# The masked key copies of a 16-wide self attention moved ahead of the query and product copies on ScalarE

## The reference

```python
q = (x @ w_q + b_q).reshape(B, Lq, 16, 16)          # x normalised; Lq = 256, B = 16
k = (context @ w_k + b_k).reshape(B, -1, 16, 16)    # 120 keys of context
v = (context @ w_v + b_v).reshape(B, -1, 16, 16)
scores = einsum('bqhd,bkhd->bhqk', q, k) / 4
weights = softmax(scores, axis=-1)
out = einsum('bhqk,bkhd->bqhd', weights, v).reshape(B, Lq, D)
x = x + out @ w_o + b_o
```

## Time and profile before

| what | us |
|---|---|
| median of three runs | 5142.15 (5141.17 to 5146.36) |
| the profiled execution's own time | 5143.89 |
| its span in the trace | 5142.0 |
| PE busy over the span | 4271.9 (83%) |
| DVE busy | 3517.8 (68%) |
| ACT busy | 2240.1 (44%) |
| POOL busy | 492.5 (10%) |
| the stage's first and last instruction in the trace | about 562 to 907 |

### The profile page before, as it was taken

How to read it: one execution, slowest core, us unless ns; L and a number is a source line. 1 busy time by engine, 2 the same in 40 slices (tenths; PEclk the granted TensorE clock), 3 DMA queues, 4 the chain that set the end, 5 groups by cost and what they waited for, 6 DMA issues and landing times. The chain is left out here.

```text
span 5142.0 us, 72988 instructions
## 1 busy us (share of the span) xinstructions
PE 4271.9 (83%) x23248; PEld 3274.5 (64%) x23248; DVE 3517.8 (68%) x8249; ACT 2240.1 (44%) x5337; POOL 492.5 (10%) x921
## 2 busy tenths in 40 slices
PE   6993588799879999999999999999514787787786
PEld 5771477577647777777777777778302555555554
DVE  4656666666667777777777777777754777777445
ACT  2331366455436555555555555655240222222322
POOL 0002100101130000000000000000301121121300
PEclk9995799899979999999999999999655888888689
DMA  2000000000000000000000000000002000000101
GB/s 59 0 0 22 33 0 0 1 0 0 12 6 1 4 1 4 3 2 4 2 4 2 4 2 4 2 2 1 3 11 59 0 0 0 0 0 0 36 0 33
DMA packets 33742, 41.23 MB, mean 8 GB/s; under 512 B 5116, under 2 KB 29954, under 8 KB 33414
## 3 DMA queue, kind: packets, MB, share of 16 engines
q1 hardware_dynamic: 33480, 38.08, 2.5%
HBM read 33.61 MB, written 4.19 MB: 7 GB/s over the span
## 5 line engine op out<-in xcount | busy, mean ns | idle before, releaser
L1563 DVE TENSOR_TENSOR global_prob_t_low<-psum,global_prob_t_high 128x512 fp32r<-128x512 f32 x960 | 657.1, 690 | 252.2 <-ACT global_prob_t_high L1655 238.0
L1655 ACT ACTIVATE global_prob_t_high<-psum 128x512 fp32r<-128x512 f32 x960 | 569.9, 601 | 586.9 <-PE psum L1769 586.9
L1569 DVE TENSOR_REDUCE global_top<-psum 128x1 f32<-128x480 f32 x1024 | 666.1, 657 | 109.2 <-PE psum L1729 104.2
L1676 ACT ACTIVATE global_prob<-psum,global_bias 128x480 f32<-128x480 f32 x1024 | 674.2, 662 | 17.9 <-DVE global_bias L1572 15.1
L1769 PE MATMUL psum<-ident,global_prob 128*128 128x128 f32 x3840 | 568.3, 273 | 37.1 <-DVE global_prob_t_low L1563 36.1
L1769 PEld LDWEIGHTS psum<-ident,global_prob 128*128 128x128 f32 x3840 | 467.4, 141 | 196.1 <-DVE global_prob_t_low L1563 68.7
L1727 PE MATMUL psum<-global_prob_t_high,global_v_low 128*128 128x512 f32 x960 | 455.7, 475 | 0.9
L1727 PE MATMUL psum<-global_k_high,global_q_low 128*128 128x480 f32 x1024 | 390.2, 381 | 15.6 <-ACT global_prob L1676 13.1
L1729 PE MATMUL psum<-global_k_high,global_q_high 128*128 128x480 f32 x1024 | 391.3, 382 | 0.0
L1728 PE MATMUL psum<-global_k_low,global_q_high 128*128 128x480 f32 x1024 | 388.3, 379 | 0.0
L1728 PE MATMUL psum<-global_prob_t_low,global_v_high 128*128 128x512 f32 x960 | 379.4, 395 | 0.0
(11 more groups left out here) (439 smaller groups left out, 8147.2 us busy)
## 6 DMA issues: line engine op xcount, KB each, us to landing
x_res<-in_x SPq DMA_DIRECT2D x4, 1024.0 KB, 9.6
moe_we<-in_expert_t SPq DMA_DIRECT2D x8, 512.0 KB, 7.6
out<-x_res SPq DMA_DIRECT2D x4, 1024.0 KB, 8.7
cho_wqkv<-in_L_ffn_Wqkv SPq DMA_DIRECT2D x2, 1536.0 KB
self_ctx_t<-in_ctx_t SPq DMA_DIRECT2D x2, 1440.0 KB
sel_w<-in_L_xattn_W SPq DMA_DIRECT2D x2, 1024.0 KB, 11.9
global_ctx_t<-in_ctx_t SPq DMA_DIRECT2D x1, 1440.0 KB
sel_ctx_t<-in_ctx_t SPq DMA_DIRECT2D x1, 1440.0 KB
```

Of the source, the lines that this page charges most:

```text
L1563: dve.tensor_tensor(dst, psum, high.bitcast(F32), ALU.subtract).then_inc(ready.sem, 1)
L1569: ins = dve.tensor_reduce(top[:, c:c + 1], w.psum[:, c, 0:chunk], AX.X, ALU.max)
L1655: act.activation(dst, psum, ACT.Copy).then_inc(ready.sem, 1)
L1676: act.activation(prob[:, par, j, c * chunk:(c + 1) * chunk], w.psum[:, c, 0:chunk], ACT.Exp, bias=bias[:, j % 2:j % 2 + 1], scale=scale, a ...
```

## The change

On ScalarE, in odd turns, the wait for `k_psum` and the four key copies (L437) with their signal `k_ready` move from behind the copy of the product (L431) to directly behind the exponential (L420), ahead of the wait for `q_psum` and the two query copies (L426) and ahead of the wait for `share_psum` and L431. No instruction is added, removed or given another shape, and no other engine's program changes.

```diff
                         act.activation(prob[:, s, :, :, :, :].rearrange("p m r a j -> p r m (a j)"),
                                        w.psum[:, 0:groups, 0:cols * NCTX].rearrange("p r (m c) -> p r m c", m=parts),
                                        ACT.Exp, scale=scale).then_inc(exped.sem, 1)
+                    if s == 1 and exists(3):
+                        act.wait_ge(k_psum.sem, k_psum.count(batch + 2))
+                        for m in range(parts):
+                            for a in range(pair):
+                                last = act.activation(k_t[:, m, a, :], kv_cols[:, m * NCTX:(m + 1) * NCTX],
+                                                      ACT.Identity, bias=bk_masked[:, m, a:a + 1],
+                                                      scale=mask[:, a:a + 1])
+                        last.then_inc(k_ready.sem, 1)
                     if exists(3):
                         act.wait_ge(q_psum.sem, q_psum.count(t + 3))
...
                         act.wait_ge(share_psum.sem, share_psum.count(t + 1))
                         act.activation(attn_raw[:, :, :], attn_cols.rearrange("p (k t) -> p k t", t=P),
                                        ACT.Copy).then_inc(attn_kept.sem, 1)
-                    if s == 1 and exists(3):
-                        act.wait_ge(k_psum.sem, k_psum.count(batch + 2))
-                        for m in range(parts):
-                            for a in range(pair):
-                                last = act.activation(k_t[:, m, a, :], kv_cols[:, m * NCTX:(m + 1) * NCTX],
-                                                      ACT.Identity, bias=bk_masked[:, m, a:a + 1],
-                                                      scale=mask[:, a:a + 1])
-                        last.then_inc(k_ready.sem, 1)
```

## The result

| | before | changed |
|---|---|---|
| median, us | 5142.11 (5141.17 to 5146.36, 5 runs) | 5121.01 (5118.20 to 5122.57, 5 runs) |
| profiled execution's span, us | 5142.0 | 5119.4 |
| PE busy over the span, us | 4271.9 | 4265.7 |

The ratio is 0.9957 (95% interval 0.9942 to 0.9971): 21 us faster by the medians, 22.6 us by the two spans. The forecast was 5118.2 us with a range of 5112 to 5126.

What follows compares the result with a forecast made beforehand. PE was taken to bound the stage, waiting 2.02 us a pass for key copies. Savings of 20.4 + 1.53 + 0.58 + 1.37 = 23.9 us took the median from 5142.15 to 5118.2 us, range 5112 to 5126.

Steps and rivals of the forecast that it cites:

- The wait and its size: PE's scores L467 wait for key copies L437 once each loop pass, 2.02 us each, 28.3 us in 14 waits.
- How long the blocks last: ScalarE's key copies start 0.337 us apart, so first key copy to first query copy takes 1.35 us.
- A pass: In a loop pass PE's scores start 1.57 us sooner (bounds 1.53 and 1.71), leaving some 0.45 us wait for queries.
- The ends of the stage: Turns outside the thirteen regular ones: turn 27 saves 1.53 us, turn -1 0.58 us, turn -3 1.37 us.
- Turn -3: Stage's start, no exponential: key copies fit before the queries, which wait for L534 as before; saves 1.37 us.
- turn -1: Near the stage's start, where the queries had waited for nothing: scores start at 594.63 against 595.21, saving 0.58 us.
- What is later than before: Queries come 0.97 us later, product copy L431 and DVE's L388 0.10 us later, with 5.3 us of cover remaining.
- The sum: Savings over 16 key-making turns: 20.4 + 1.53 + 0.58 + 1.37 = 23.9 us.
- B: Rival: PE's whole 2.02 us wait before the scores goes, 32.2 us saved, 5110 us; chance 0.03.
- C: Rival: key copies stretch beside PE's PSUM writes, or branch and registers hold PE's scores, losing part; chance 0.09.
- D: Rival: no effect, because the queries come as late as the keys did, about 5142 us; chance 0.01.
- E: Rival: slower, because PE idles less and its clock falls to 1.2 GHz for part of the stage; chance 0.01.

Runs made afterwards that it cites:

- spare copies out of SBUF: Changed kernel plus four copies of a constant into an unread tile, between keys and queries in odd turns: ratio 1.0003 to before, pass 20.39 us.
- product between: Changed kernel with the queries moved behind the product's copy in all turns (keys, product, queries): ratio 0.9998 to before, passes of 20.70 us.
- spare copies behind: Changed kernel plus four copies of a constant into an unread tile, behind the product's copy: ratio 0.9951 to before, pass 18.90 us.
- two without repeated waits: Changed kernel without PE's second exponential wait (L480), or also without its second transposed-probabilities wait (L525): ratios 0.9949 and 0.9955 to before.
- By halves: Changed kernel making two key copies and one query copy per part, PE waiting per half of L467: ratio 0.9931 to before, pass 18.43 us.
- shares first: Version making keys and queries by part, with PE's share transposes and their wait moved ahead of L544: ratio 0.9930 to before, pass 18.27 us.

## Why the prediction was right

**The wait and its size.** Right. The 2.02 us in each pass became 0.42, and 2.02 was all idle time that nothing else would have filled: both other engines had room, as DVE's shrinking wait shows.

**How long the blocks last.** The row of the kernel before gave 1.35 us for four key copies, and 1.35 it was (839.83 - 838.48). The estimate by the Trainium skill ("ScalarE: Activation LUTs", section What ACT_TABLE_LOAD costs), 1.52 us, was too long for this copy, and close to what the spare copies out of SBUF took, 1.51.

**A pass.** Predicted saving 1.57 us, measured 22.4 / 14 = 1.60. The chain from the exponential's start to the scores was to be 3.83 us and is 3.80. The step from the queries' end to PE was taken as 0.20 and is 840.61 - 840.48 = 0.13; in exchange the two query copies took 0.65 us and not 0.62.

**The ends of the stage.** Turn -3 was put at 1.37 us and gave 1.3 (the step from the queries' end to PE was 575.50 - 575.36 = 0.14 us and not 0.05), turn -1 at 0.58 and gave 0.6. Turn -2 was not in the sum and gave 0.7: L534 took 1.16 us there against 2.08 before, because PE's granted clock had risen from 1.2 to 2.4 GHz a few matmuls sooner, 12.6 us behind the stage's first matmul and not 16.9. This is luck of the execution as far as the runs show. Five kernels have PE's program in common here, and PE's times up to the first of these moments: the clock rose after 12.6 us in the changed kernel, 13.6 with the product between (L534 took 1.27 us), and about 10 with the spare copies behind and in the two without repeated waits. The scores behind turn -2 started 15.4, 15.8 and 14.6 us behind the first matmul accordingly. By halves and with the shares first, whose starts are also equal, it rose after 14.8 and 13.8 us. What decides the moment is open; no run isolates it.

**What is later than before.** The product's copy was to come 0.10 us later against L549, and L388 with it. L388 starts 840.78 - 839.75 = 1.03 us behind the shares' start where it was 0.89: 0.14. It is covered.

**The sum.** 23.9 us were forecast for the stage, 24.9 measured, the missing 1.0 being turn -2 and 0.03 us a pass, of which the first is luck. The median came out 21.1 us lower, 2.8 us above the forecast time. The profiled executions lost 2.3 us outside the stage, where nothing was changed. That this comes from the executions is inferred from the spread of the traces there; the kernel before has only one trace, and all ten others came to the stage later than it, by 1.3 to 3.4 us.

**The rivals.** B (the whole wait goes) was right in its mechanism and not reached: two key copies fewer, or a split by halves, take the last 0.5 us. C did not come: the key copies last 0.458 us beside PE's matmuls as before. D did not come: the queries were never as late as the keys had been. With the product between, the kernel is as slow as before, but by waits in both turns and not by this one. E did not come: the clock stayed at 1.00 with PE busy 96.25 of 100 us, and at 98.4 in the version by halves.

## What to carry to other kernels

When an engine at its limit waits for two products of another engine, the wait ends with the last of them, so list the whole chain of copies from their common start to that wait, take out of it everything that is wanted later, and put first what has its input first. Time on the other engine has different prices by place: four copies that nobody waits for cost 1.48 us a pass ahead of the queries and nothing behind the product. So what is awaited goes first, even though it then delays the other product, and what is not awaited goes last. Once the order is right, the next step is to hand over by parts: the consumer's first half needs only the first part of each.

## What the runs showed of the hardware that was not expected

- A wait on a register's value that is already fulfilled costs PE next to nothing: taking one away ahead of L480 left a pass at 18.90 us, and one put in between the sixteen matmuls of L467 cost 0.01 us. Where the same wait was not yet fulfilled (shares first), the weight loads behind it stood 0.25 us and the sixteen matmuls took 1.25 us instead of 1.10.
- The gaps of 0.17 to 0.30 us that the profile puts down to issue stand where the weights' block goes to or from 32 rows or 32 columns: 0.30 from 32 rows to 120 or 128 columns of 128 rows (L480, L525), 0.20 from 32 columns to 128 x 128, 0.17 from the shares to 32 rows or 32 columns, 0.20 from 32 columns to 32 rows. From the queries to 32 columns it is 0.11 to 0.12 us. A change between 96 and 128 rows shows at most 0.08 us (L480 to L489). With the shares beside the queries, both 128 x 128, there is none. Only this one move was tried, so it is shown for the shares and inferred for the others.
- PE's granted clock rose from 1.2 to 2.4 GHz at moments 9.9 to 13.6 us behind the stage's first matmul in five executions with the same program of PE and the same times until the first of them. In a stage of 340 us this moved the scores behind turn -2 by 1.2 us.
- A masked copy of 128 x 120 with bias and scale by partition repeats every 0.34 us from PSUM, lasting 0.46, and every 0.38 us from a constant tile in SBUF, lasting 0.50.
